# A decoder layer on one core: the mixer's matrix products as three float32r products of split operands, attention products untiled

## What is computed

```python
x = x + _L0_attn_ref(_layernorm(x), ...)   # the mixer
#   proj = einsum('bld,td->blt', xn, W_in)       z, xi (1024 each), dt (16), B, C (256 each)
#   xi = silu(causal conv of 4 taps over xi);  dt = softplus(dt + bias)
#   h = exp(dt*A) * h + dt*mean(xi)*B  over time;  y = sum(h*C)
#   out = einsum('bli,di->bld', (y @ W_h2i.T) * silu(z), W_out) + residual
x = x + _L0_xattn_ref(_layernorm(x), ctx_512, ctx_512)   # 32 query heads, 8 key heads, width 16
x = x + _L0_ffn_ref(_layernorm(x), ...)     # shared expert + the top 2 of 16 experts
```

## Time and profile before

| | us |
|---|---|
| median of 3 runs | 1221.38 (1219.46 to 1221.67) |
| the profiled execution | 1216.94 |
| its span, first to last instruction | 1215.1 |
| batch 0's mixer | from about 15 to 125 |
| batch 1's mixer before slot 0 | 125 to 186 |
| attention slots 0 to 255 | about 184 to 890 |
| routed experts | from about 898 on |
| PE, DVE, ACT, POOL busy | 1168.5, 691.5, 475.3, 386.6 |

### The profile page before, as it was taken

One profiled execution on the slowest core, in us unless ns is written; L12 is line 12 of the kernel. 1 busy time (PEld: TensorE's weight loads), 2 busy tenths in 40 slices (PEclk: granted clock), 3 DMA queues, 4 the chain that ended last, 5 costly groups with the idle time before them and its releaser, 6 DMA issues. The chain is left out here.

```text
span 1215.1 us, 31305 instructions
## 1 busy us (share of the span) xinstructions
PE 1168.5 (96%) x13185; PEld 581.4 (48%) x13186; DVE 691.5 (57%) x1150; ACT 475.3 (39%) x669; POOL 386.6 (32%) x502
## 2 busy tenths in 40 slices
PE   6999999999999999999999999999999999999997
PEld 3444434444545544545645554444444444444443
DVE  3833595756787665668675777877657222222221
ACT  3320324533555453545453455555632222222222
POOL 5212311221321330231122121110102576777775
PEclk9999999999999999999999999999999999999999
DMA  8321874104384201364500245200135676678640
GB/s 205 103 80 32 190 161 120 29 15 120 69 162 85 72 25 28 84 118 105 112 20 16 68 105 93 83 3 3 72 114 166 171 188 138 142 225 233 182 83 2
DMA packets 119603, 122.24 MB, mean 101 GB/s; under 512 B 25472, under 2 KB 84992, under 8 KB 119344
## 3 DMA queue, kind: packets, MB, share of 16 engines
q1 hardware_dynamic: 101744, 98.59, 31.6%
q0 software_dynamic: 17008, 21.16, 9.0%
q10 hardware_dynamic: 720, 0.61, 0.2%
HBM read 94.63 MB, written 40.77 MB: 111 GB/s over the span
## 5 line engine op out<-in xcount | busy, mean ns | idle before, releaser
L683 DVE TENSOR_REDUCE mx<-ps_m 128x2 f32<-128x1024 f32 x256 | 313.0, 1223 | 193.6 <-PE ps_m L1024 189.3
L892 ACT ACTIVATE prob<-ps_s 128x1024 f32<-128x1024 f32 x256 | 262.0, 1023 | 322.7 <-PE ps_s L1024 321.7
L1024 PE MATMUL acc<-xnT,wring 128*32 128x512 f32 x1888 | 249.0, 592 | 0.6 <-DVE first_z L619 0.6
L1869 PE MATMUL ps_gu<-ring,xgT 128*128 x376 | 176.7, 593 | 1.0 <-DVE xgT L1573 1.0
L1508 POOL DMA_INDIRECT out<-y,dest x92 | 143.7, 1562 | 77.5 <-ACT y L1734 60.4
L1024 PE MATMUL ps_s<-q_stack,k_stack 99*32 99x512 bf16 x2048 | 161.7, 380 | 4.4 <-ACT prob L892 3.8
L1024 PE MATMUL ps_m<-k_stack,q_stack 96*32 96x512 bf16 x1952 | 153.2, 380 | 9.8 <-DVE mx L683 8.2
L1573 DVE COPY xgT<-ps_x 128x512 f32<-128x512 f32 x47 | 32.5, 692 | 202.1 <-PE ps_x L1839 202.1
L1209 PE MATMUL ps_o<-prob,values 128*32 128x128 f32 x4096 | 138.4, 273 | 0.0
L1209 PEld LDWEIGHTS ps_o<-prob,values 128*32 128x32 f32 x4096 | 116.3, 110 | 44.7 <-issue 39.2
L1024 PEld LDWEIGHTS ps_m<-k_stack,q_stack 96*32 96x32 bf16 x1952 | 55.6, 96 | 127.3 <-issue 72.8
(11 more groups left out here) (282 smaller groups left out, 1201.6 us busy)
## 6 DMA issues: line engine op xcount, KB each, us to landing
ring<-in_w_experts SPq DMA_DIRECT2D x96, 256.0 KB, 4.7
wring<-in_w_in SPq DMA_DIRECT2D x80, 256.0 KB, 4.2
q_stack<-part_rows SPq DMA_DIRECT2D x96, 128.0 KB, 4.6
wring<-in_w_out SPq DMA_DIRECT2D x32, 256.0 KB, 2.9
part_rows<-part SPq DMA_DIRECT2D x20, 384.0 KB, 3.8
out<-x SPq DMA_DIRECT2D x4, 1024.0 KB, 4.8
xt<-in_x SPq DMA_DIRECT2D x14, 256.0 KB, 4.6
k_stack<-part_rows SPq DMA_DIRECT2D x48, 64.0 KB, 3.0
```

Source lines behind the costliest of these rows:

```text
L683: nc.vector.tensor_reduce(mx[:, n % G, 2 * u:2 * u + 2], ps_m[:, :, :], AX.X, ALU.max).then_inc(s_max, 1)
L892: nc.scalar.activation(prob[:, slot % PROB, :, :], ps_s[:, :, :], ACT.Exp, scale=SCALE).then_inc(s_exp, 1)
L1024: ins = nc.tensor.matmul(dst[c:c + 32, :], stationary[:, c:c + 32], moving, start=start, stop=stop, tile_position=(0, c))
L1869: ins = nc.tensor.matmul(ps_gu[p][:, :], xgT[:, p, k * P:(k + 1) * P], weights(own)[:, k * 2 * F:(k + 1) * 2 * F], start=(k == 0), stop=(k ...
```

## The change

- `split_product`: each projection and out-projection product becomes three float32r matmuls, high x high, high x low and low x high, on 128x128 without tiling, where `high` is a value rounded to float32r and `low` the rest.
- `product` never tiles any more: the bfloat16 scores, heads-to-inner, `outputs` and the shared expert's products are one 128x128 matmul each. Only probabilities times values, and the small 32-column products, stay tiled. `project_steps` (dt) reads both pieces of the activations as float32, so it has 32 products instead of 16.
- Activations: ACT writes `xnT_high` in four 128x128 steps per token tile (`evacuate_high`), then DVE `xnT_low` in four (`evacuate_low`), where DVE made one 128x512 step. The gated blocks are copied by ACT (`high_gated`, m = 44 to 48) and the rest subtracted by DVE (even blocks, m = 45 to 48) and POOL (odd blocks, m = 46 to 49).
- Weights: in batch 0 ACT and POOL split each of the 28 blocks, SP stores the 512 KB pair to DRAM (`w_pieces`). Later batches load pairs. The ring holds 5 pairs. The out-projection of batches 1 to 3 runs its token tiles in two pairs (0,1) and (2,3), so it loads its 8 blocks twice.
- `add_x1` moves to m = 54, 55, 62, 63 in batches 1 to 3 and 60 to 63 in batch 0. Statistics follow one slot later. `prob` has 4 buffers instead of 6. `gated_high` lies over `bsb`, `csb`, `state` and `gains`, so the next batch's writes to those wait for the end of the out-projection.
- Start: statistics and the power step run in two halves, the first residual moves from ACT to DVE, and cutting the heads-to-inner weights is spread over m = 9 to 17.

```diff
-    RING = 10
+    RING = 5
+    RAW = 10
-    PROB = 6
+    PROB = 4
...
+        X1_AT = ((60, 61, 62, 63), (54, 55, 62, 63), (54, 55, 62, 63), (54, 55, 62, 63))
...
+            def store_pieces(w):
+
+                sp.wait_ge(s_wlow, w + 1)
+                sp.dma_start(dram["w_pieces"][w], pieces[:, w % RING, :, :].bitcast(F32)).then_inc(s_wst[w % RING], 16)
+                if w + RAW < PIECES:
+                    load_raw(w + RAW)
...
+            def low_gated(b, i):
+
+                pool.wait_ge(s_ghigh[1], 4 * b + i // 2 + 1)
+                nc.gpsimd.tensor_tensor(gated_low[i], gated[i], gated_high[:, i, :], ALU.subtract
+                                        ).then_inc(s_glow[1], 1)
...
+            def high_weights(w):
+
+                act.wait_ge(s_raw[w % RAW], 16 * (w // RAW + 1))
+                if w >= RING:
+                    done, value, _ = consumed(0, w - RING)
+                    act.wait_ge(done, value)
+                    act.wait_ge(*stored(w - RING))
+                nc.scalar.activation(pieces[:, w % RING, 0, :], raw[:, w % RAW, :], ACT.Copy).then_inc(s_whigh, 1)
...
-                if not tiled[0]:
-                    return nc.tensor.matmul(dst, stationary, moving, start=start, stop=stop)
-                for c in range(0, P, 32):
-                    ins = nc.tensor.matmul(dst[c:c + 32, :], stationary[:, c:c + 32], moving, start=start, stop=stop,
-                                           tile_position=(0, c))
-                return ins
+                return nc.tensor.matmul(dst, stationary, moving, start=start, stop=stop)
+
+            def split_product(dst, stationary, moving, start, stop):
+
+                product(dst, stationary[0], moving[0], start, False)
+                product(dst, stationary[0], moving[1], False, False)
+                return product(dst, stationary[1], moving[0], False, stop)
...
             def project_out(b, j, i):
-                w = BLOCKS * b + GROUPS - 1 + i
+                if i == 0:
+                    if j % 2:
+                        pe.wait_ge(s_icopy, 4 * b + (3 if b == 0 and j == 1 else 4))
+                    else:
+                        pe.wait_ge(s_gate, 4 * b + (3 if b == 0 and j == 0 else 4))
+                    if b and j >= 2:
+                        pe.wait_ge(s_x1, TB * b + j - 1)
                 if j == 0:
...
+                    pe.wait_ge(s_glow[i % 2], 4 * b + i // 2 + 1)
+                weights = weights_there(b, out_block(b, j, i))
```

More of the change, by code:

```diff
@@ L11 @@
 BF16 = mybir.dt.bfloat16
+F32R = mybir.dt.float32r
 ALU = mybir.AluOpType
@@ L134, in stream_phase @@
         gated = [first_z[:, 0, :], first_z[:, 1, :]] + [xz[:, i, :] for i in range(2, KI)]
+        gated_low = [first_z_low[:, 0, :], first_z_low[:, 1, :]] + [xz_low[:, i, :] for i in range(2, KI)]
         q = xz[:, TB:, :]
@@ L352, in _ @@
                         load_x(b + 1)
-                    if m >= 4 and m % 2 == 0 and m // 2 - 2 < GROUPS - 1:
-                        freed(b, m // 2 - 2)
+                    for w in range(blocks(b)):
+                        if consumed(b, w)[2] == m:
+                            freed(b, w)
+                    if b == 0:
+                        for w in range(PIECES):
+                            if (w if w < RING else SPLIT_AT[w] + 2) == m:
+                                store_pieces(w)
                     if m == 9:
@@ L484, in _, with ones_of_keys @@
             pool.wait_ge(s_p, steps.n)
-            deviations(0)
-            cut_head_weights()
-            nc.gpsimd.memset(k_stack[KQ:KM, :, :], 1.0).then_inc(s_ones, 1)
-            pool.wait_ge(s_ones, 1)
+            def ones_of_keys(half):
+                nc.gpsimd.memset(k_stack[KQ:KM, G // 2 * half:G // 2 * (half + 1), :], 1.0).then_inc(s_ones, 1)
+                pool.wait_ge(s_ones, half + 1)
+            ones_of_keys(0)
+            first_deviations(0)
+            first_deviations(2)
+            pool.wait_ge(s_rs, 2)
+            ones_of_keys(1)
+            for w in range(RING):
+                low_weights(w)
             for slot in span:
@@ L857, in _ @@
                         if m in TURN_AT:
-                            evacuate(b + 1, TURN_AT.index(m))
+                            evacuate_low(b + 1, TURN_AT.index(m))
                 for j in range(TB):
-                    if (a := batch_at(slot, -41 + 4 * j)) is not None:
-                        attention_statistics(a, j)
+                    for a in range(B):
+                        if mixing(slot - 1) == (a, X1_AT[a][j]):
+                            attention_statistics(a, j)
                 if (a := batch_at(slot, -28)) is not None:
@@ L923, in _ @@
             nc.scalar.activation(neg_a[:, :], neg_a[:, :], ACT.Copy, scale=-1.0).then_inc(s_nega, 1)
-            act.wait_ge(s_keep, 1)
+            act.wait_ge(s_const, 16)
             for j in range(TB):
-                nc.scalar.activation(x1[:, j, :], xt[:, j, :], ACT.Identity, bias=keep[:, j, 1:2], scale=keep[:, j, 0:1]
-                                     ).then_inc(s_kept, 1)
+                evacuate_high(0, j)
+                if j == 1:
+                    high_weights(0)
+            for w in range(1, RING):
+                high_weights(w)
             for slot in span:
@@ L1005, in _ @@
                                          ).then_inc(s_icopy, 1)
+                if b < B and 44 <= m <= 48:
+                    for i in (2 * (m - 44), 2 * (m - 45) + 1):
+                        if 0 <= i < KI:
+                            high_gated(b, i)
+                if b == 0:
+                    for w in range(RING, PIECES):
+                        if SPLIT_AT[w] == m:
+                            high_weights(w)
+                if b + 1 < B and m in TURN_AT:
+                    evacuate_high(b + 1, TURN_AT.index(m))
                 if u == 5 and 0 <= n + 1 < N:
@@ L1277, in _ @@
                 n, u = divmod(slot, UNITS)
-                tiled[0] = slot >= 0
                 if 0 <= slot < SLOTS:
```

302 lines of the change are left out of this document (195 added, 107 removed).

## The result

The changed kernel takes 1251.21 us (median of 4 runs, 1248.83 to 1253.94) where the kernel before takes 1221.00 in the same comparison: the ratio is 1.025, with a 95% interval of 1.0226 to 1.0274. It is slower by 30 us. The forecast was 1187 with a range of 1158 to 1214, so both the direction and the range were wrong.

The account below looks back on a forecast made before the run. PE's pace was taken as the bound, except where DVE fills a slot. Stage gains 10.3 + 2.0 + 15.8 + 11.4 - 6.9 + 2 = 34.6 us took the median from 1221.4 to about 1187, range 1158 to 1214.

Parts of the forecast that it names:

- The core: Mixer products: a float32r matmul of 512 columns takes 0.215 us, a product 0.645 instead of 0.86; 448 save 96.3 us.
- The rival on the weights' load: Each float32r matmul: loading its float32 weights sets the pace; at 0.30 the time is 1301 us; chance 0.09.
- Going between tiled and whole: PE in every pair of slots: switching costs 0, upper bound 0.05 us a pair, 6 us in all.
- The rival that said so: Each change of tiling drains PE: 0.16 us for each of 2 x 128 changes, 41 us, giving 1228; chance 0.04.
- Loss (1): Out-projection, batches 1 to 3: PE's second product waits for `first_z_low` behind POOL's last gatings, -4.0 us a batch.
- Loss (2): Out-projection, batches 1 to 3: PE waits for `add_x1` at m = 54 and again at 55, -2.0 us each.
- the waits don't bite: Out-projection waits and chains: other slack absorbs them and PE's list sets the time, giving 1159 us; chance 0.15.
- Batch 0: Before 15.45 to 125.1 us: gross gain 23.2, less 12.9 for start, chains, xi blocks and gating, net 10.3 us.
- DVE's last xi blocks: Batch 0: a loss of 0.8 us at these blocks, as PE's products shrink.
- Batch 1 before slot 0: A stretch of 61 us: gross gain 10.3, reduced by DVE's pace in pairs and by DMA, net 2.0 us.
- the DMA rival: DMA becomes the bound: ACT's high pieces wait for stores, batches 1 to 3 in the out-projection; 28 us, 1215; chance 0.12.
- After the last mixer: Slots 164 on: maxima and exponentials set the pace, whole products end slightly earlier; gain 2 us, bounds -2 and 4.

Follow-up runs that it names:

- the first experiment: The kernel before with only its float32 mixer and bfloat16 score and maxima products made whole beside attention, no float32r: 1235.27 us, ratio 1.0127.

## Why the prediction was wrong, step by step

- **The core: "I take 0.215".** A float32r matmul takes 0.233 alone and 0.238 beside bfloat16. A product costs 0.70 to 0.71, not 0.645, and 448 of them save 67 to 72 us instead of 96.3: 24 to 29 were missing from the first term, less where DVE hides it. The row that I leaned on shows float32 as four streams; nothing in it says that a float32r stream runs as fast. The rival on the weights' load named the right row to watch, "a pace of 0.24", and the pace stayed under it, but not for its reason. Of the two bounds named, 0.215 and 0.43, the price is near the lower, not at it.
- **Going between tiled and whole: "I take 0, with an upper bound of 0.05 a pair".** It is 0.24 a pair, and 16.2 us in the whole program (the first experiment). This is the step that failed as reasoning. I read the earlier trace rows as untiled transposes between tiled products. They are of the form 128*12, and in after, where going between whole and tiled shows (0.32 from the float32r matmul at 443.75 to the first of them), one of them starts 0.05 behind a `ps_o` product and is followed by the next after 0.06 (444.19, 444.24, 444.30). So nothing is paid between the two, and they say nothing of whole products. The only whole products of full width in before lay before slot 0, where nothing was tiled. So no row bore on it, and the bound had to be taken from elsewhere. The rule of the Trainium skill ("TensorEngine Tiling (Array Packing)", Key Properties), that changing the mode drains the engine, is what the trace agrees with, in that every change costs time (0.10 in, 0.14 out). The rival that said so had 0.32 a pair, a third too much, and a chance of 0.04, far too little.
- **Loss (1), `first_z_low` on POOL: 4.0.** The wait is 3.8, at the place and for the reason forecast. The slot grew by 5.4, 6.8 and 6.8.
- **Loss (2), `add_x1`: twice 2.0.** Both holes are 1.96. The three slots grew by 6.0 to 7.5 over the 7.98 without the waits.
- **The clock is missing from both.** PE was at 2.4 GHz in before up to its last 2 us, so no row of before showed a lower one. After eight of these nine waits PE ran for some microseconds at 1.2 GHz. Waits forecast at 8.0 a batch took 12.8 to 14.3, 40 us in the three batches: 16 for the clock. (The run without them was 35 faster.) For the same reason the rival "the waits don't bite" priced at 24 us what was worth about 35.
- **Batch 0: net 10.3.** It came out as -13 (from the dt products at 16.35 to those of batch 1 at 139.02: 122.7 us against 109.7). Before's batch 0 took 109.7 to 112.4 in the five profiles with the same code there, so -13 is the far end of -10 to -13. The chain before `outputs` was right: 6.0 us waited, with "about 6 us" forecast. What I left out is GpSimd beside VectorE: 28 low pieces of 1.3 us and the cuts, spread over the stretch where VectorE is fullest. Shorter low pieces brought 6 us back, so it is a part of the miss of 20 to 23. The clock is another: 0.95 over 71 us and 0.87 over 39 in the stages of after make up to 8.6 us, where before had 1.00. What the two leave stays open. I sized the residual steps that moved to VectorE by nothing, and "DVE's last xi blocks" at 0.8, where PE waited 7.0 for the first taps. The rows of before could have warned: DVE is busy for 9.8 and 9.7 of 10 us from 35 to 55 there, but not what POOL does to it.
- **Batch 1 before slot 0: 2.0.** It came out as -1 (60.4 us from its dt products to slot 0, with 59.3 before).
- **DMA.** No wait of PE names the reloaded `pieces` in after, at 0.50 of DMA share in slots 0 to 63. Placing them at nothing was right, and that half of the DMA rival was wrong. In batch 0, at 0.80, ACT waited for stores of `w_pieces` for 3.3 us in all (15 to 130 us of after), not the 14 that the rival had; what of it reached PE, no run tells.
- **After the last mixer: +2.** It is -2.7 for slots 192 to 255, the same passing between modes; tiled again from slot 164 on, 5.4 us come back.
- **The range.** The costs that decided are 24 to 29 for the pace, 16 for the passes, 16 for the clock behind the waits and 20 to 23 in batch 0. They overlap, since batch 0 holds a quarter of the products, so they do not add up to the 64 us between 1187 and 1251. Each had a bound of a few us or none at all. The high end took in one rival at a time.

Of the list "What will show it": the starts are 0.233 to 0.238 apart, not 0.215; the pairs at m = 28 to 41 take 5.67, not 5.2; the waits of 4, 2 and 6 us are as forecast. Neither sign of being wrong, a pace above 0.24 or waits for `pieces`, was seen, and the prediction was wrong all the same: no sign stood for the passes, for the clock or for GpSimd beside VectorE.

## What to carry to other kernels

A matmul that is cheaper alone must be priced in its place: if it forces whole products between tiled ones, count the passes, here 0.24 us for going and coming back. A wait on the matrix engine costs more than its length when the granted clock is low behind it: a wait of 3.8 us made its slot 5.4 to 6.8 longer. Take such waits out before counting a gain; moving the sums by one slot and four steps a batch to another engine was worth 35 us here. Work given to GpSimd in a stretch where VectorE is full can make VectorE's steps several times longer (2.4 instead of 0.54): place it beside steps that read PSUM, and look at the same step's duration in other places of the trace.

## What the runs showed of the hardware

- A float32r matmul of 128x128 by 512 columns: 0.233 us from start to start, 0.12 for 256 columns; bfloat16 whole or tiled, and each of float32's four streams, 0.215. The weight load of 0.19 does not limit it.
- Whole to 32-column products and back: +0.10 and +0.14 us beside float32; 0.3 to 0.4 for both, between tiled bfloat16 or 32-column products and whole float32r.
- The granted clock fell to 1.2 GHz at holes of 3.1, 4.8 and 7.0 us between two matmuls in a kernel without float32r, and at most of 2.3 and 4.2 in after. It was low for 3 to 10 us and stayed at 2.4 behind a hole of 1.5. The length alone did not decide: holes of 2.1, 2.3 and once 4.1 were followed by 2.4 GHz in some places.
- A VectorE step over 4 columns lasted 4.35 us beside GpSimd, 0.18 without it; one with two SBUF inputs 3.69 instead of 0.68; taps, which read PSUM, stayed at 0.73 to 0.75.
